# Cross-attention to 257 keys: weighted values of two batches in one run, scores waited for in halves, second half copied first

## The reference

```python
x = x + xattn(_layernorm(x, axis=-1), ctx_1024, ...)
def xattn(xq, xkv, Wq, Wkv, Wout, bout):
    q = (xq @ Wq.T).reshape(B, SQ, NUM_HEADS, HEAD_DIM)
    kv = (xkv @ Wkv.T).reshape(B, SKV, 2, NUM_HEADS, HEAD_DIM)
    k, v = (kv[:, :, 0], kv[:, :, 1])
    att = jax.nn.softmax(jnp.einsum('bxhd,byhd->bhxy', q, k) * scale, axis=-1)
    x = jnp.einsum('bhxy,byhd->bxhd', att, v).reshape(B, SQ, H)
    return x @ Wout.T + bout
```

## Time and profile before

| | |
|---|---|
| median of 3 runs | 3991.93 us (3991.15 to 3996.01) |
| profiled execution, its own time | 3982.57 us |
| its span, first to last instruction | 3980.8 us |
| busy, share of the span | PE 85%, PEld 62%, DVE 67%, ACT 59%, POOL 61% |
| exponentials of each stage (L2477) | 512, 472 ns each, 238.8 us; idle ahead of them 111 to 114 us |
| first halves of `a_cross`: all of E scaled (L2251) | 128, 1900 ns each |
| context, 32 transfers in each stage | 578.0 KB each, 3.7 us to landing |

### The profile page before, as it was taken

One profiled execution on the slowest core, in us unless ns is written; L12 is line 12 of the kernel. 1 busy time (PEld: TensorE's weight loads), 2 busy tenths in 40 slices (PEclk: granted clock), 3 DMA queues, 4 the chain that ended last, 5 costly groups with the idle time before them and its releaser, 6 DMA issues. The chain is left out here.

```text
span 3980.8 us, 119953 instructions
## 1 busy us (share of the span) xinstructions
PE 3385.2 (85%) x44674; PEld 2469.3 (62%) x44674; DVE 2670.8 (67%) x7002; ACT 2362.3 (59%) x6308; POOL 2422.3 (61%) x2724
## 2 busy tenths in 40 slices
PE   7999959999999579698698999978499999786866
PEld 5777737777777467365466777745277777453444
DVE  6888757777777523477445888857778887754655
ACT  6777736666666334386124777745577777644633
POOL 6767656776777343574425887746367676845733
PEclk9999979999999689898799999989599999887968
DMA  2111110000000122101221111110011111000023
GB/s 75 36 42 36 36 70 6 8 11 11 8 6 2 63 72 77 47 14 47 67 72 59 51 45 42 37 60 4 17 37 36 42 36 30 3 2 6 2 93 94
DMA packets 90549, 149.05 MB, mean 37 GB/s; under 512 B 10112, under 2 KB 66816, under 8 KB 89664
## 3 DMA queue, kind: packets, MB, share of 16 engines
q1 hardware_dynamic: 79936, 122.87, 9.9%
q0 software_dynamic: 10240, 20.99, 1.7%
HBM read 112.76 MB, written 31.06 MB: 36 GB/s over the span
## 5 line engine op out<-in xcount | busy, mean ns | idle before, releaser
L2251 POOL TENSOR_TENSOR t_cross_E<-t_cross_E,t_cross_inverse 128x1028 f32<-128x1028 f32 x128 | 243.2, 1900 | 134.8 <-DVE t_cross_inverse L2530 134.8
L2251 POOL TENSOR_TENSOR a_cross_E<-a_cross_E,a_cross_inverse 128x1028 f32<-128x1028 f32 x128 | 243.2, 1900 | 132.8 <-DVE a_cross_inverse L2530 132.8
L2477 ACT ACTIVATE t_cross_E<-t_cross_psum,t_cross_negtop 128x257 f32<-128x257 f32 x512 | 238.8, 472 | 113.5 <-DVE t_cross_negtop L2520 110.0
L2477 ACT ACTIVATE a_cross_E<-a_cross_psum,a_cross_negtop 128x257 f32<-128x257 f32 x512 | 238.8, 472 | 112.4 <-DVE a_cross_negtop L2520 103.9
L2477 ACT ACTIVATE e_cross_E<-e_cross_psum,e_cross_negtop 128x257 f32<-128x257 f32 x512 | 238.8, 472 | 111.2 <-DVE e_cross_negtop L2520 103.3
L2251 POOL TENSOR_TENSOR e_cross_E<-e_cross_E,e_cross_inverse 128x1028 f32<-128x1028 f32 x128 | 243.2, 1900 | 94.2 <-DVE e_cross_inverse L2530 94.1
L3090 PEld LDWEIGHTS l_psum<-l_ffn_w,l_hidden 128*128 128x128 f32 x1536 | 197.9, 192 | 98.0 <-issue 56.1
L3090 PE MATMUL l_psum<-l_ffn_w,l_hidden 128*128 128x128 f32 x1536 | 207.8, 278 | 19.0 <-POOL l_hidden L2963 17.9
L3083 PE MATMUL l_psum<-l_hT,l_ffn_w 128*128 128x512 f32 x384 | 200.6, 625 | 0.9 <-ACT l_hT L3139 0.9
L2520 DVE TENSOR_REDUCE t_cross_negtop<-t_cross_psum 128x2 f32<-128x514 f32 x256 | 175.8, 687 | 32.6 <-PE t_cross_psum L2337 31.7
L2520 DVE TENSOR_REDUCE a_cross_negtop<-a_cross_psum 128x2 f32<-128x514 f32 x256 | 175.4, 686 | 26.8 <-PE a_cross_psum L2332 26.4
(11 more groups left out here) (754 smaller groups left out, 11124.1 us busy)
## 6 DMA issues: line engine op xcount, KB each, us to landing
a_cross_context<-context SPq DMA_DIRECT2D x32, 578.0 KB, 3.7
e_cross_context<-context SPq DMA_DIRECT2D x32, 578.0 KB, 3.7
t_cross_context<-context SPq DMA_DIRECT2D x32, 578.0 KB, 3.7
u_moe_weights<-pack_u_moe SPq DMA_DIRECT2D x1, 5633.0 KB, 16.3
slots<-l_blank SPq DMA_DIRECT2D x6, 832.0 KB, 12.2
a_moe_x_slots<-slots SPq DMA_DIRECT2D x26, 192.0 KB, 2.8
slots<-a_moe_y_slots SPq DMA_DIRECT2D x26, 192.0 KB, 2.1
c_moe_x_slots<-slots SPq DMA_DIRECT2D x26, 192.0 KB, 2.8
```

The lines of the kernel that those rows point to most:

```text
L2251: pool.tensor_tensor(E[:, n % N], E[:, n % N], spread(inverse[:, n % 4], SK, 2), ALU.mult).then_inc(s_unit, 1)
L2477: act.activation(E[:, n % N, g], psum[:, g, 0:SK], ACT.Exp, bias=negtop[:, n % 2, g:g + 1], accum_out=total[:, n % 2, g:g + 1]).then_inc(s ...
```

## The change

All of it is in `cross_attention`, so it acts in all three stages:

1. ET has four buffers (n % 4) instead of two; the copies into it wait for the values of four batches before.
2. PE does `values` for batches n-4 and n-3 together, in the steps with even n, and none in the odd ones.
3. `scores` is issued in two halves (banks 0 and 1; banks 2 and 3). Each half waits for the exponentials of the same half of batch n-1 alone and raises `s_score` by itself; DVE's two maxima wait for a half each. In `t_cross` the mask matmuls of a half follow it.
4. On ACT, `second_half(n-3)` comes first in the step, ahead of `begin` and `values_out`.

No instruction of computation is added or removed.

```diff
--- before.py
+++ after.py
@@ -2147,7 +2147,7 @@
         qT = sc.sb("qT", [P, 2, P])
         q_heads = sc.sb("q_heads", [P, 2, BPT, J, S])
         E = sc.sb("E", [P, N, G, SK])
-        ET = sc.sb("ET", [P, 2, 2, G * P])
+        ET = sc.sb("ET", [P, 4, 2, G * P])
         last_of = sc.sb("last_of", [P, 2, BPT, 2, G, J])
         E_last = sc.sb("E_last", [LAST, BPT, S])
         negtop = sc.sb("negtop", [P, 2, G])
@@ -2325,18 +2325,19 @@
                 pe.wait_ge(s_k, i * N + n + 1)
                 if n % 4 == 0:
                     pe.wait_ge(s_heads, i * 2 + n // 4 + 1)
-                if exists(i, n - 1):
-                    pe.wait_ge(s_exp, (i * N + n) * G)
-                for g in range(G):
-                    rows = slice(g * 32, (g + 1) * 32)
-                    last = pe.matmul(psum[:, g, 0:SK], q_heads[rows, n // 4 % 2, n % 4].rearrange("p j s -> p (j s)"),
-                                     kT[rows, n % 2], start=True, stop=mask is None)
-                if mask is not None:
-                    for g in range(G):
+                for half in range(2):
+                    if exists(i, n - 1):
+                        pe.wait_ge(s_exp, (i * N + n - 1) * G + 2 * half + 2)
+                    for g in (2 * half, 2 * half + 1):
                         rows = slice(g * 32, (g + 1) * 32)
-                        last = pe.matmul(psum[:, g, 0:SK], fold_bf[rows].rearrange("p j s -> p (j s)"), mask_neg[rows],
-                                         start=False, stop=True)
-                last.then_inc(s_score, 1)
+                        last = pe.matmul(psum[:, g, 0:SK], q_heads[rows, n // 4 % 2, n % 4].rearrange("p j s -> p (j s)"),
+                                         kT[rows, n % 2], start=True, stop=mask is None)
+                    if mask is not None:
+                        for g in (2 * half, 2 * half + 1):
+                            rows = slice(g * 32, (g + 1) * 32)
+                            last = pe.matmul(psum[:, g, 0:SK], fold_bf[rows].rearrange("p j s -> p (j s)"), mask_neg[rows],
+                                             start=False, stop=True)
+                    last.then_inc(s_score, 1)
 
             def side(i, n):
 
@@ -2398,7 +2399,7 @@
                 for c in range(2):
                     for g in range(G):
                         last = pe.matmul(psum[g * 32:(g + 1) * 32, O_BANK, n % 4 * P:(n % 4 + 1) * P],
-                                         v_sb[:, n % N, c, g * 32:(g + 1) * 32], ET[:, n % 2, c, g * P:(g + 1) * P],
+                                         v_sb[:, n % N, c, g * 32:(g + 1) * 32], ET[:, n % 4, c, g * P:(g + 1) * P],
                                          start=(c == 0), stop=(c == 1))
                 last.then_inc(s_pv, 1)
 
@@ -2414,8 +2415,9 @@
                     project_values(i, n + 1)
                 if exists(i, n - 2):
                     turn(i, n - 2, 1)
-                if exists(i, n - 3):
-                    values(i, n - 3)
+                for m in (n - 4, n - 3):
+                    if n % 2 == 0 and exists(i, m):
+                        values(i, m)
 
             turn_normed(0, 0)
             queries(0, 0)
@@ -2462,9 +2464,9 @@
 
             def second_half(i, n):
                 act.wait_ge(s_t1, i * N + n + 1)
-                if exists(i, n - 2):
-                    act.wait_ge(s_pv, i * N + n - 1)
-                act.activation(ET[:, n % 2, 1], psum[:, K_BANK], ACT.Copy).then_inc(s_ET1, 1)
+                if exists(i, n - 4):
+                    act.wait_ge(s_pv, i * N + n - 3)
+                act.activation(ET[:, n % 4, 1], psum[:, K_BANK], ACT.Copy).then_inc(s_ET1, 1)
 
             def values_out(i, n):
                 act.wait_ge(s_vp, i * N + n + 1)
@@ -2478,11 +2480,11 @@
                                    accum_out=total[:, n % 2, g:g + 1]).then_inc(s_exp, 1)
 
             def step(i, n):
+                if exists(i, n - 3):
+                    second_half(i, n - 3)
                 begin(i, n - 1)
                 if exists(i, n):
                     values_out(i, n)
-                if exists(i, n - 3):
-                    second_half(i, n - 3)
                 side_out(i, n - 1)
                 if exists(i, n):
                     exponentials(i, n)
@@ -2514,16 +2516,15 @@
                 dve.tensor_scalar(mask_neg[:], mask_int[:], 0.0, -1e30, ALU.is_equal, ALU.mult).then_inc(s_mask_ready, 1)
 
             def maximum(i, n, half):
-                if half == 0:
-                    dve.wait_ge(s_score, i * N + n + 1)
+                dve.wait_ge(s_score, (i * N + n) * 2 + half + 1)
                 at = slice(2 * half, 2 * half + 2)
                 dve.tensor_reduce(negtop[:, n % 2, at], psum[:, at, 0:SK], AX.X, ALU.max, negate=True).then_inc(s_top, 1)
 
             def first_half(i, n):
                 dve.wait_ge(s_t0, i * N + n + 1)
-                if exists(i, n - 2):
-                    dve.wait_ge(s_pv, i * N + n - 1)
-                dve.tensor_copy(ET[:, n % 2, 0], psum[:, T_BANK]).then_inc(s_ET0, 1)
+                if exists(i, n - 4):
+                    dve.wait_ge(s_pv, i * N + n - 3)
+                dve.tensor_copy(ET[:, n % 4, 0], psum[:, T_BANK]).then_inc(s_ET0, 1)
 
             def reciprocals(i, n):
                 dve.wait_ge(s_exp, (i * N + n) * G + G)
```

## The result

The changed kernel takes 4078.66 us (median of 4 runs, 4072.57 to 4084.15) against 3991.54 us: a ratio of 1.0215, with a 95% interval of 1.0198 to 1.0231. It is slower, by 87 us; 4080 was forecast. Its profiled execution took 4084.15 us, with a span of 4082.2 us.

The account below looks back on a forecast made before the run. The prediction took a ring of scores, maximum and exponentials, with DVE waiting for ACT's copies, as the bound. Four steps gave + 0.92 us per tile, + 88 us over 3982.6, plus 9.4 to the median: 4080 us, range 4020 to 4130.

Parts of the forecast that it names:

- a ring of DVE, ACT and PE: Cross stages: scores, maximum, exponentials and back to the next scores bound the step, with no engine full; 15.13 us per tile.
- Batch 1 to 2: First maximum to first maximum: last_weights waits for values_out, delayed 0.48 us by the ET copy; 4.21 us, from 3.82.
- Batch 2 to 3: First maximum to first maximum: the picks wait for begin, delayed 0.48 us by the ET copy; 4.45 us, from 4.10.
- Batch 0 to 1: First maximum to first maximum: no ACT copy awaited, paired values hold the next scores on PE; 3.48 us.
- Batch 3 to 0: First maximum to first maximum: last_values waits for values_out; 3.81 us, on average 3.91 with the loop turn, from 3.57.
- The sum: Four steps of a tile: 16.05 us against 15.13, + 0.92, times 32 tiles and 3 stages: + 88 us.
- the first rival: Less slow: the pair does not hold batch 1, that step 2.85 instead of 3.48 us; 4020 us, chance 0.11.
- Pairs: PE's values of two batches in even steps: matter only from batch 0 to 1; odd-step saving lies under waits.
- Halves: Scores split on PE: DVE cannot use the earlier half, as the reciprocal stands ahead of the maximum; extra semaphore taken as 0.
- Late keys: Slower rival: in odd steps keys miss DVE by a further 0.25 us in two of four steps; 4128 us, chance 0.10.
- The faster case: Rival: DVE's waits stay covered and PE sets the step, returning 147 us; 3845 us, chance 0.04.
- The clock: Rival: PE's clock falls to 1.2 GHz, slowing scores and keys in one step of eight; 4130 us, chance 0.02.

Follow-up runs that it names:

- e1: Kernel before with only ACT's second_half moved ahead of begin and values_out: 4068.79 us against 3991.87.
- e6: Kernel before with second_half moved ahead only in ACT's step of batch 1 of each tile: 3989.73 us against 4004.63.
- e7: Kernel before with second_half moved ahead only in ACT's steps of batches 2, 3 and 0: 4094.07 us against 4004.63.
- e4: Kernel before with only the scores waited for in halves, each maximum waiting for its half: 3993.02 us against 3991.87.
- e3: Kernel before with four ET buffers and values in pairs, whole scores, ACT's old order: 4034.38 us against 3991.87.
- e5: Changed kernel with ACT's order begin, second_half, values_out: 4057.65 us against 4004.63 for the kernel before.
- e2: Changed kernel with ACT's old order (second_half last), pairs, halves and four buffers kept: 4041.52 us against 3991.87 for the kernel before.

## Why the prediction was right

**The bound.** It named a ring of DVE, ACT and PE in which an instruction of DVE waits for a copy of ACT in three of four steps. e1, e6 and e7 show it: the same copy, moved ahead in the steps where DVE waits, costs 89 us, and in the one where it does not, it gains 15. DVE's idle time ahead of `last_weights` came as said (over 1 us), that ahead of `last_values` at 0.99.

**Batch 1 to 2**, 4.21 forecast, 4.20 and 4.09 measured. The 0.48 us of ET came in whole (202.34 to 202.81 is 0.47), `last_weights` 0.43 behind the start of `values_out`. The rows shown are of the second tile, 4.08 us long: there M is 0.51 behind `last_weights` instead of the 0.59 I took, and the last exponential starts 2.22 us after M, so the keys were late by 0.04 and not by 0.10. **Batch 2 to 3**, 4.45 forecast, 4.44 measured, each term within 0.02. **Batch 0 to 1**, 3.48 forecast, 3.49 and 3.57 measured. Two errors cancel in it: two batches of values took 1.08 us, where 0.64 + 0.38 = 1.02 was taken, and the transposes began 0.05 us after the keys copy (213.44 to 213.49), where 0.17 was taken.

**Batch 3 to 0** was mis-sized where the loop turns: 4.16 instead of 4.02. The reciprocal came 0.51 us after `last_values` (211.72 to 212.23, "0.23 <-issue"), where I took the 0.42 of the earlier trace rows. This is the price of the halves on DVE that e4 shows, and the working had none; in e1, which has no halves, the step takes 4.05. At 0.1 us in each of the 48 turns it is an estimated 5 us. In the other tile 3.82 was measured and 3.81 forecast.

**The sum** was + 0.92 us for a tile and is + 0.89 by the steps' means; + 88 us forecast, 87 by the medians and 80 by the stages. The base was wrong: 484.3 us from the first to the last maximum are 127 steps and the 0.6 us to the last batch's second maximum, and not 128 steps. So a tile takes 15.23 us, as the means of the steps say (15.22), and not 15.13. With that base the same steps give + 0.83 and + 80 us, 4072 in all. That error raised the forecast by some 8 us, and the steps, 0.06 us a tile too short in all, lowered it by 6; that they nearly cancel, and that the forecast fell within 2 us of the median, is luck. (In the first rival, 2.18 + 0.47 + 0.10 + 0.08 is 2.83 and not 2.85; nothing hangs on it.)

**The three stages** were given the same + 29 us each; they took 26.4, 22.9 and 30.3. The mask matmuls of `t_cross` were taken as covered. In the changed kernel the step 0 to 1, the one in which M waits for the scores, takes 3.59 and 3.74 us there, against 3.49 and 3.57 in `a_cross`, so in this step they are not. Why `e_cross` loses least was not looked into.

**Pairs** were given one step too few. The working had them hold only batch 0 to 1; e3 shows that they also hold the picks in 2 to 3, by 0.41 us. In the changed kernel `begun` comes later still, by 0.26 us (4.44 against e5's 4.18), so the omission happened to do no harm to the sum. With the copy's order undone (e2) this step alone is 0.42 and 0.47 us longer than before, which over 96 tiles is 43 of the 46 us of the stages. The prediction asked what is late next and answered ACT's copies; in this step it would have been PE's pair.

**Halves** were said to be useless since DVE's reciprocal stands ahead of M. In the changed kernel they are issued apart in odd steps, as said, and take 0.70 us each, 1.40 in all where the whole took 0.72:

```profile
210.00 0.70 PE L2333 MATMUL a_cross_psum<-a_cross_kT,a_cross_q_heads 32*128 32x257 f32 x4
...
210.97 0.70 PE L2333 MATMUL a_cross_psum<-a_cross_kT,a_cross_q_heads 32*128 32x257 f32 x4 [0.27 <-ACT a_cross_E L2479]
```

But the reason given was too strong. Without the copy first, e4 shows two steps of eight about 0.2 us shorter: the reciprocal is ready early enough there, and M had waited for the scores. What cancels the gain is the keys copy behind M, later by 0.22 us. Late keys were given as a rival with a further loss; in e4 they are where the gain goes.

**The rivals.** The range held. The pair does hold batch 1: M waits 0.53 us "<-PE" there. The faster case needed DVE's waits to stay covered; they were not. The clock did not fall: 1.00 in 60 to 483.8 us before and after, with waits of PE of up to 0.7 us in both. The Trainium skill, "TensorE: Matmul & The Clock Gate", section "Loop structure matters more than you think", has the clock fall where a long wait for DMA stands between every matmul. The waits in this stretch are short and for other engines, so they neither show this nor speak against it.

**What stays open.** Whether DVE's waits could be shortened at their root, by waiting for PE's write (`s_vp`) and not for ACT's copy, was not tried: DVE and ACT would then read one PSUM bank at a time. The Trainium skill, "PSUM — Partial Sum Buffer", section "PSUM bank collisions raise a hardware error", says that two engines on the same bank and partitions raise an error even where both only read; no run here shows it. The copy first with halves but without pairs was not run, so what the pairs cost inside the changed kernel is open. The four ET buffers were never run without the pairs; the prediction put them at nothing. Moving those results to another bank was not tried either.

## What to carry to other kernels

Before an instruction is moved forward on an engine, list who waits for what it overtakes: a move that costs its own engine nothing still delays the signal of each instruction that it overtakes, here by its own 0.48 us. Where the pattern of waits repeats over four steps, decide for each step by itself; the same copy ahead of its neighbours gained 15 us in one step and cost 89 in the others. And when two edits both lengthen the same step, price each alone and each as taken out of the whole: 77 and 42 us made 87 together, and undoing the copy gave back 37 and not 77. Last, when a length is divided by a count, count the gaps and not the events: 128 maxima have 127 steps between them.

## What the runs showed of the hardware

Where PE goes from one use of the array to another (the whole of it, strips of rows, strips of columns), the next loads come late. Two groups that both use the whole array, `project_values` and the transposes of the kernel before:

```profile
203.37 0.61 PE L2320 MATMUL a_cross_psum<-a_cross_weights,a_cross_context 128*128 128x128 f32 x4
...
203.70 0.47 PEld L2390 LDWEIGHTS a_cross_psum<-const_sb,a_cross_E 128*128 128x128 f32 x4
```

The loads start 0.28 us before the end of the matmuls in flight. From the transposes to the values' strips of columns they start 0.07 us before it (203.81 + 0.60 against 204.34), and from these to the scores' strips of rows in the changed kernel 0.07 (214.07 + 1.08 against 215.08). Ends of matmuls are modelled in the profile, so these are differences of records and not of the array itself.

Two of four row strips take as long as all four: 0.70 us for a half of the scores alone, 0.72 to 0.76 (215.08) for both halves in a row.

Where the loop turns, after eight batches, DVE's reciprocal starts 0.41 us after `last_values` without halves and 0.52 with them, against 0.21 in the tile that does not end the turn. The branch is what stands there and not in the other tile; no run took it away.
